# Two recurrent layers on one core: mixes 0 and 1, and 2 and 3, computed as pairs on two strips of rows, half of the output at a time

## What is computed

```python
xa = _ln(x, ln1_w, ln1_b)
sx = jnp.concatenate([state[:, 1:2] - xa[:, :1], xa[:, :-1] - xa[:, 1:]], axis=1)
xxx = jnp.tanh((xa + sx * maa_x) @ maa_w1).reshape(b, l, 5, DM)      # DM = 32
xxx = jnp.einsum('blfd,fde->blfe', xxx, maa_w2)                      # the five mixes
xm = xa[:, :, None] + sx[:, :, None] * (maa_stack + xxx)
xk, xw, xv, xr, xg = (xm[:, :, j] for j in range(5))
w = jnp.exp(-jnp.exp(time_decay + jnp.tanh(xw @ td_w1) @ td_w2)).reshape(b, l, h, s_)
r, k, v = (y @ W.T for y, W in ((xr, Wr), (xk, Wk), (xv, Wv)))
g = jax.nn.silu(xg @ Wg.T)
def step(s, rkvw):
    r_t, k_t, v_t, w_t = rkvw
    a = k_t[..., :, None] * v_t[..., None, :]
    out = jnp.einsum('bhi,bhij->bhj', r_t, u * a + s)
    return a + w_t[..., :, None] * s, out
```

## Time and profile before

| | us |
|---|---|
| median of 3 runs (lowest to highest) | 3081.06 (3078.34 to 3083.32) |
| the profiled execution, its own time | 3076.93 |
| its span | 3075.0 |
| PE busy / DVE busy / ACT busy / POOL busy | 2811.2 / 2003.5 / 1350.9 / 665.0 |
| PE matmuls at L523 (the mixes), 640 records | 133.8 |
| mean granted TensorE clock | 0.962 of full |

### The profile page before, as it was taken

One profiled execution on the slowest core, in us unless ns is written; L12 is line 12 of the kernel. 1 busy time (PEld: TensorE's weight loads), 2 busy tenths in 40 slices (PEclk: granted clock), 3 DMA queues, 4 the chain that ended last, 5 costly groups with the idle time before them and its releaser, 6 DMA issues.

```text
span 3075.0 us, 53764 instructions
## 1 busy us (share of the span) xinstructions
PE 2811.2 (91%) x18112; PEld 2186.9 (71%) x18112; DVE 2003.5 (65%) x4888; ACT 1350.9 (44%) x3446; POOL 665.0 (22%) x436
## 2 busy tenths in 40 slices
PE   7999999967999999779999999999997889999986
PEld 7555555856888888666555455799996768888866
DVE  2878787338999999644555556511101699999993
ACT  1888888542443443343444444332311234444432
POOL 0111110015444444300000000000000454444440
PEclk9999999978999999889999999999998899999998
DMA  2100100313333333300000000300002333333340
GB/s 107 36 24 34 34 23 13 130 41 98 92 92 90 88 91 92 107 27 10 30 20 19 26 22 10 126 26 1 0 1 89 92 95 92 89 92 92 87 126 14
DMA packets 96167, 182.85 MB, mean 59 GB/s; under 512 B 10122, under 2 KB 87498, under 8 KB 92462
## 3 DMA queue, kind: packets, MB, share of 16 engines
q1 hardware_dynamic: 96046, 181.27, 19.2%
HBM read 171.34 MB, written 9.90 MB: 59 GB/s over the span
## 4 chain that ended last, share of the span: by engine, by line
PE 66%; DVE 12%; issue 9%; ACT 8%; DMA 2%; POOL 1%; SPq 0%; DVEq 0%; ACTq 0%; POOLq 0%
PE psum L509 19%; PE psum L314 10%; PE psum L1859 6%; PE psum L1746 4%; PE psum L1303 3%; DVE psum L708 3%; PE psum L500 3%; ACT arena L1506 3%; ACT arena L2126 2%; PE psum L1759 2%; PE psum L1801 2%; PE psum L516 2%; PE psum L1315 2%; DVE arena L723 2%; PE psum L523 2%
## 5 line engine op out<-in xcount | busy, mean ns | idle before, releaser
L509 PE MATMUL psum<-arena 128*128 128x200 f32 x4096 | 772.1, 347 | 51.5 <-DVE arena L876 18.6
L509 PEld LDWEIGHTS psum<-arena 128*128 128x128 f32 x4096 | 721.9, 198 | 135.6 <-issue 79.3
L1107 POOL TENSOR_TENSOR arena<-arena 128x800 f32<-128x800 f32 x256 | 454.9, 1780 | 452.2 <-DVE psum L708 452.2
L723 DVE TENSOR_TENSOR_SCAN arena<-arena,psum 128x808 f32<-128x808 f32 x256 | 470.0, 1836 | 37.3 <-PE psum L500 22.1
L314 PE MATMUL psum<-arena 128*128 128x200 f32 (+1 forms) x1920 | 332.1, 335 | 15.0 <-POOLq L139 13.3
L314 PEld LDWEIGHTS psum<-arena 128*128 128x128 f32 x1920 | 328.5, 192 | 16.7 <-POOLq L139 13.3
L1506 ACT ACTIVATE arena<-arena 100x361 f32<-100x361 f32 x512 | 300.6, 590 | 87.2 <-DVE arena L1417 85.5
L1087 POOL TENSOR_TENSOR arena<-arena 128x800 f32<-128x800 f32 x80 | 140.6, 1757 | 807.6 <-DVE arena L731 632.3
L708 DVE TENSOR_TENSOR psum<-arena 128x808 f32<-128x808 f32 x256 | 280.6, 1096 | 5.5
L1417 DVE CUSTOM_DVE_ANT_0 arena<-psum,arena 100x361 f32<-100x361 f32 x512 | 254.3, 531 | 45.4 <-ACT arena L1506 37.9
L1303 PEld LDWEIGHTS psum<-arena 100*128 100x128 f32 x1536 | 146.3, 142 | 131.2 <-ACT arena L1518 60.3
(11 more groups left out here) (142 smaller groups left out, 3908.3 us busy)
## 6 DMA issues: line engine op xcount, KB each, us to landing
arena<-v_rows SPq DMA_DIRECT2D x512, 202.0 KB, 3.2
arena<-ctxT SPq DMA_DIRECT2D x32, 722.0 KB, 4.2
arena<-L_w SPq DMA_DIRECT2D x9, 1024.0 KB, 10.5
arena<-L_w SPq DMA_DIRECT2D x8, 1152.0 KB, 16.1
v_rows<-arena SPq DMA_DIRECT2D x32, 202.0 KB, 2.1
arena<-L_fc SPq DMA_DIRECT2D x4, 1024.0 KB, 8.3
arena<-L_pj SPq DMA_DIRECT2D x4, 1024.0 KB, 15.5
arena<-xT SPq DMA_DIRECT2D x4, 800.0 KB, 12.0
```

Source lines behind the costliest of these rows:

```text
L509: mm = pe.matmul(chunk(bank, j), m.W[n][:, k, c * P:(c + 1) * P], src[:, k, :], start=k == 0, stop=k == C - 1)
L723: dve.tensor_tensor_scan(m.ring[n % 4].rearrange("p j e -> p (j e)"), m.we[:, cc].rearrange("p j e -> p (j e)"), m.kv, 0.0, ALU.mult, ALU. ...
L1107: pool.tensor_tensor(sv, sv, rb, ALU.mult).then_inc(sem("r_states"), 1)
```

## The change

Mixes 0 and 1 are computed together, and so are 2 and 3. The first call of a pair makes chunks 0 and 1 of both inputs, the second call chunks 2 and 3 of both. Its four matmuls alternate between the two inputs, hence between two strips of 32 rows; those of the even input go into bank 4, those of the odd one into bank 5. `mix_term` follows: each call finishes two chunks of each of two inputs. So the sixth term is the last of input 0, the eighth the last of input 1, the fourteenth that of input 2 and the sixteenth that of input 3, and `add_token` waits for those counts. Two waits on DVE move to the earlier call, since it now writes into both inputs. The fifth mix keeps its old form under the name `last_mix`.

```diff
             def mix(x):
 
-                w, th, r0 = (m.w2, m.tha, DM * x) if x < 4 else (m.low, m.thl, BACK)
+                for j in range(2):
+                    for n in range(2):
+                        r0, c = DM * (x - x % 2 + n), 2 * (x % 2) + j
+                        mm = pe.matmul(chunk(4 + n, j), m.w2[r0:r0 + DM, c * P:(c + 1) * P], m.tha[r0:r0 + DM, :],
+                                       start=True, stop=True)
+                mm.then_inc(sem("mix_sum"), 1)
+
+            def last_mix():
+
                 for c in range(C):
-                    mm = pe.matmul(chunk(4 + c // 2, c % 2), w[r0:r0 + DM, c * P:(c + 1) * P], th[r0:r0 + DM, :],
-                                   start=True, stop=True)
+                    mm = pe.matmul(chunk(4 + c // 2, c % 2), m.low[BACK:BACK + DM, c * P:(c + 1) * P],
+                                   m.thl[BACK:BACK + DM, :], start=True, stop=True)
                 mm.then_inc(sem("mix_sum"), 1)
...
-                mix(4)
+                last_mix()
...
                 wait(dve, "mix_sum", f, x + 1)
-                for c in range(C):
-                    dve.scalar_tensor_tensor(m.xm[x][:, c, :], chunk(4 + c // 2, c % 2), vec(f"stack{x}", c),
-                                             m.sx[:, c, :], ALU.add, ALU.mult).then_inc(sem("mix_term"), 1)
+                for n in range(2):
+                    for j in range(2):
+                        c, y = (2 * (x % 2) + j, x - x % 2 + n) if x < 4 else (2 * n + j, x)
+                        dve.scalar_tensor_tensor(m.xm[y][:, c, :], chunk(4 + n, j), vec(f"stack{y}", c),
+                                                 m.sx[:, c, :], ALU.add, ALU.mult).then_inc(sem("mix_term"), 1)
...
                     wait(dve, "k_sum", i, 2)
+                    wait(dve, "decay", i, 4)
                 mix_term(0)
...
-                if rec:
-                    wait(dve, "decay", i, 4)
                 mix_term(1)
...
                     wait(dve, "v_sum", i, 2)
+                    wait(dve, "r_sum", i, 2)
                 mix_term(2)
...
-                if rec:
-                    wait(dve, "r_sum", i, 2)
                 mix_term(3)
...
             def add_token(x):
-                wait(pool, "mix_term", f, 4 * x + 4)
+                wait(pool, "mix_term", f, (6, 8, 14, 16, 20)[x])
                 pool.tensor_tensor(seq(m.xm[x]), seq(m.xm[x]), m.xs[:, :, :, 1:E], ALU.add).then_inc(sem("mixed"), 1)
```

## The result

| | before | with the change |
|---|---|---|
| median, us (lowest to highest) | 3082.19 (3078.34 to 3084.07), 4 runs | 3189.82 (3188.0 to 3193.62), 4 runs |
| profiled execution, own time / span | 3076.93 / 3075.0 | 3189.13 / 3187.2 |
| mean granted clock | 0.962 | 0.941 |

The change is **3.5% slower**: ratio 1.0352, 95% interval 1.0335 to 1.037. The forecast was 3208 us, range 3157 to 3250.

The account below looks back on a forecast made before the run. PE and DVE, both nearly full in the recurrent loop, were taken to be bound by their hand-over order. Per body 6.84 + 2.2 + 0.6 = 9.6 us; 115 plus 12 for first bodies gave +127, 3208 us, range 3157 to 3250.

Parts of the forecast that it names:

- +0.6: Gap before "v, half 0" grows to 4 or 5 us: half rate costs 0.6 us more per full body.
- 2.2 for the new one: New PE gap before "k, half 0": the half-rate clock behind it costs 2.2 us per full body.
- The lower bound, 1.7: Low end of the 1.7 to 2.8 us half-rate cost forecast for a PE gap of about 4.7 us.
- brings forward ... 0.45 us: Shorter `mix(0)` brings the "o, half 1" sum forward, removing DVE's 0.45 us wait at L835.
- Two signs of the forecast: In the new profile: a loop of about 88 us, and scan 12 waiting 6 us or more for L500.
- layer 3 repeats the pattern: Layer 3 has layer 1's clock pattern: four of a layer's six full bodies have a half-rate stretch.
- 3 us for each of these four: First two bodies of each recurrent layer: 3 us later each, 12 us together.
- the 4.1 us added for the median: Median of the runs taken as 4.1 us above the profiled execution, turning 3204 into 3208 us.
- no clock loss: Rival: gaps appear but both projections run at full rate, or few bodies fall; 3157 us, chance 0.10.
- The strips don't overlap: Rival: `mix(2)` on PE stays at 1.55 us and DVE's L835 wait stays; 3221 us, chance 0.06.
- Only one hand-over is late: Rival: the second shift hides behind the first, leaving 3.85 us per body; 3135 us, chance 0.05.
- Faster: Rival: DVE runs far enough ahead that adds wait for nobody and PE saves 2.6 us per body; 3045 us, chance 0.03.

Follow-up runs that it names:

- The counts alone: Kernel before, with only POOL's token adds waiting for 6, 8, 14, 16 and 20 terms; 3216.43 us, ratio 1.0435.
- The filled gaps: The change plus ten and fourteen useless matmuls in PE's gaps before "k, half 0" and "v, half 0", 12 full bodies; 3150.73 us, ratio 1.0223.
- the pairs taken alone: The change with one pair, the other as in the kernel before: mixes 0 and 1 paired 3141.63 us (1.0186); mixes 2 and 3 paired 3147.19 us (1.0200).
- the order without the clever part: Fastest reordered kernel (DVE terms between product and scan, mixes 2, 3 and reduce 4 earlier on PE) without pairs; 3064.04 us, ratio 0.9936 against the kernel before.

## Why the prediction was right, and where its sizes were off

The mechanism was the one forecast, in both places: the token adds become late, PE's next projection stands behind each in PE's order, and DVE's scan 12 carries the delay into the next body. The counts alone reproduce it. Term by term, for one full body (bodies 3 to 6 of a layer, the one read in the earlier trace rows and above):

| term | forecast, us | measured, us | from |
|---|---|---|---|
| one mix | 0.90 | 0.88 | 1069.50 to 1070.38 |
| `mix_term` start to token add | 0.91 | 0.83 | 1062.30 to 1063.13 |
| variance to the norm's scale | 5.28 | 5.13 | 1070.38 to 1075.51 |
| half rate behind the first gap | 2.2 | 1.69 | 4.66 against 2.97 |
| `mix_term(1)` to "v, half 0" in all | 18.30 | 17.30 | 1062.30 to 1079.60 |
| "v, half 0" to `reduce(4)`, against before | +0.6 | -0.16 | 4.42 against 4.58 |
| `reduce(4)` to `mix_term(1)`, against before | -0.45 | -1.37 | see below |
| body | +9.6 | +6.95 | 85.35 against 78.40 |

Two terms were mis-sized in the body. The clock is the first: "2.2 for the new one" and "+0.6" came to 1.69 and -0.16. The lower bound, 1.7, fits both (1.69, and 4.42 less 2.90, 1.52), since each stretch ended with its projection and did not reach `mix(2)` and the variance. The filled gaps give 3.25 us per body for both together, as I expected after seeing the profile.

The second is "brings forward ... 0.45 us". The stretch from `reduce(4)` to `mix_term(1)` became 1.37 us shorter. 0.45 of it is the wait at L835, which is gone. 0.82 is the copy behind the centring: 0.99 us before, 0.17 after. The remaining 0.1 I did not follow. The copy and POOL's product in the kernel before, and the copy with the counts alone:

```profile
1027.50 0.99 DVE L842 COPY arena<-arena 128x8 f32 x1
1026.71 1.75 POOL L1107 TENSOR_TENSOR arena<-arena 128x800 f32<-128x800 f32 x1
```

```profile
1072.59 0.17 DVE L842 COPY arena<-arena 128x8 f32 x1
```

Before, POOL's product ran to 1028.46, and the copy ended at 1028.49. With the change and with the counts alone POOL stands idle at that moment. The count run moves nothing else, and its copy takes 0.17 us. Over the twelve traced kernels there are 192 such copies: the 72 that started during an operation of POOL ended 0.03 to 0.04 us behind it and took 0.34 to 1.05 us, the other 120 took 0.16 to 0.17. So a late token add also clears the way for this copy, which the prediction did not see. It is most of why the gap in front of "k, half 0" is 3.70 us and not 4.7.

Two signs of the forecast did not come true: the loop is 85.35 us and not 88, and scan 12 waits 4.62 us for L500 and not 6 or more. Of the latter, 1.1 us is the product of step 12, which took 2.10 us instead of 1.00 beside POOL. And "layer 3 repeats the pattern" was true (granted clock 1.00, then 0.98 there too), but the earlier trace rows show layer 1 alone.

Then the first bodies. I took "3 us for each of these four". PE's timeline of body 0 with the change:

```profile
725.37 5.70 PE L509 MATMUL psum<-arena 128*128 128x200 f32 x16 [2.15 <-POOL arena L1095]
...
739.45 5.59 PE L509 MATMUL psum<-arena 128*128 128x200 f32 x16 [4.88 <-POOL arena L1095]
```

"v, half 0" starts at 739.45 instead of 727.99. Both projections ran at half rate there (5.70 and 5.59 us for 16 records). Where each body of layer 1 begins, taken at the projection (L509) ahead of its `mix(0)`:

| | before, us | with the change | late by | the body's own share |
|---|---|---|---|---|
| body 1 | 782.08 | 793.42 | 11.3 | 11.3 for bodies -1 and 0 |
| body 2 | 859.30 | 879.73 | 20.4 | 9.1 for body 1 |
| body 3 | 936.84 | 965.15 | 28.3 | 7.9 for body 2 |
| body 4 | 1015.26 | 1050.54 | 35.3 | 7.0 for body 3 |

Bodies 3 to 6 cost 6.9 to 7.0 us each, and layer 3 shows the same within 0.4 us. So bodies -1 and 0 together cost 11 us and not 6. Bodies 1 and 2 cost more than the later ones because the kernel before had no half rate there, and its body 2 was 77.5 us long and not 78.4. In body 1 "k, half 0" also ran at half rate all through, 5.66 us instead of 4.66. Over two layers the twelve full bodies make 89 us and the first ones 22, 112 us in all, against 115 + 12 = 127 forecast and 112.2 measured on the spans. The errors, -26 and +10, partly cancel; that the total is nearer than its parts is luck. The rest of the 18 us between 3208 and 3190 is the 4.1 us added for the median, which came out only 0.7 above the profiled execution.

The rivals: "no clock loss" is refuted by the profile and priced by the filled gaps (3150.73 us; I had 3157 for it). "The strips don't overlap" is refuted by 0.88 us for a mix that took 1.55. "Only one hand-over is late" is refuted by the pairs taken alone. "Faster" needed `mix_term(1)` 3.9 us earlier against PE; moving it in DVE's order shrank PE's gap in front of "k" from 3.70 to 0.88 us, which faster matmuls alone did not. The Trainium skill's advice against idle gaps (TensorE: Matmul & The Clock Gate, section "Why this matters for your kernels") held: 3.3 of the 7 us per body came back when the gaps were filled.

## What to carry to other kernels

Before a step is made faster by pairing it with its neighbour, ask when the first of the two results is complete, and who has it as next in its order. Here two results that came one step later left PE idle for 3.70 and 5.23 us per body, and at half rate behind each gap. A few late operations are cheaper to move than to speed up: four DVE operations in front of one scan gave back 42 us, while the mixes' 44 us less on PE (133.8 to 63.7 + 25.9 us busy) gave nothing that could be measured once the order was right. And test the order without the clever part, too: here it carried the whole gain.

## What was not expected of the hardware

- The order in which the matmuls on two strips of rows are issued did not matter here: 8 records take 0.88 us alternating and 0.88 us strip by strip, against 1.55 us on one strip.
- Work that computes nothing made the kernel faster: 24 matmuls per body took 39 us off, through the granted clock (mean 0.962 instead of 0.941).
- Operations of DVE stretch where POOL is at work. Beside the copy, the products of steps 10 and 12 took 2.09 and 2.10 us with the change (0.99 and 1.00 in the kernel before), with POOL's product behind the add at 2.50 us instead of 1.75. From 800 to 1300 us, in all twelve traced kernels, every product of DVE that overlapped an operation of POOL by more than 0.1 us took 1.26 to 2.50 us, and every other one 0.99 to 1.01. The scans (1.84 us) and the mix terms (1.42) of the body read did not stretch beside POOL. No run takes the reason apart.
